# Output projection, first quarter: half of the weight splits moved into it, late ternary tiles on VectorE alone, the next piece's high part moved ahead

## The chip, the cores and the metric

The kernel runs on one core of a Trainium2 chip. The number is the device time of one execution in microseconds (us), shown as the median of several executions. A profiled execution has a time of its own and a span, which is the stretch that its trace covers.

## The reference, cut to what matters

One transformer block on x of shape (2, 1024, 512), with modulation vectors from a small conditioning input. It has two halves:

```
h = layernorm(x) * (1 + ca) + sa
q, k, v = h @ Wq, h @ Wk, h @ Wv          # 32 query heads in 8 groups, one k and v head of 64 for each group
attn = softmax(causal(rope(q) @ rope(k).T / 8)) @ v
x = x + ga * (attn @ Wo)                  # Wo: 2048 x 512, the output projection
h = layernorm(x) * (1 + cb) + sb
x = x + gb * ffn(h)                       # silu(gate) * up, rms norm, down
```

The weights of ffn are quantised to three levels first: w is cast to bf16 and cut in groups of 64; scale = max(mean |w|, 1e-8); w_hat = clip(round(w / scale), -1, 1) * scale; and what is used is w + (w_hat - w), rounded to bf16 at each step.

## The kernel before, in words

**Precision.** The large fp32 products of the attention and of the output projection are made of fp32r products on TensorE: each operand is split into a high part (a cast on ScalarE) and a low part (raw minus high, on VectorE), and high*high, high*low and low*high are added in PSUM. The three product lines of the output projection are L1433, L1434 and L1435.

**Stages.** First the attention, whose step loop runs over 8 head groups with 72 steps each; then the output projection, in four quarters of 512 rows of x; then the feed-forward. The order of work on each engine in the attention is written out by hand: tables at the top give, for each kind of work, the step and the place in the step. Each engine then takes its program strictly in that order, and engines wait for one another on semaphores.

**Splitting Wo.** Wo is 16 tiles of 128 rows, taken two at a time as weight pieces i = 0 to 7. `load_weights` (L1366, issued by SP) loads piece i into `wo_raw[:, i % 2]`, so piece i needs the low part of piece i - 2 to be done; `weights_high` (L1370, ScalarE) makes `wo_hi`, `weights_low` (L1374, VectorE) makes `wo_lo`. The two results lie where `hT_hi` and `hT_lo` were, and the trace calls them that. All eight splits are in the last head group of the attention, at the steps WO_HIGH and WO_LOW (34 to 65), and the loads of pieces 2 to 7 at WO_NEXT.

**The output projection.** A quarter has NPC = 8 pieces s of the attention's output: half i = s // 4 of its rows, and p = s % 4 of the 2048 inner columns, PIECE = 4 tiles each. `load_piece` (L1380, SP) brings a piece to one of O_RING = 4 raw buffers, `piece_high` (L1386, ScalarE) and `piece_low` (L1390, VectorE) split it into one of RING = 2 buffers. `piece_high` of piece s waits until TensorE has finished piece s - 2 (`piece_done`). TensorE does 24 matmuls for a piece (2 row tiles, 4 inner tiles, 3 products), and after pieces 1 to 6 eight transposes (L1446) of a ternary weight tile, which ScalarE copies out (L1515, `copy_turned`). Pieces 0 and 1 of the first quarter are loaded and split while the attention still runs. The first quarter is unrolled (`first`), the other three are a hardware loop. TensorE's first matmul waits for `wo_ready` = 8, all the weights. After half of a quarter VectorE adds the residual (L1536, L1538).

**The late ternary tiles.** The feed-forward's weights are quantised in units of 128x512 beside the attention, six for each head group. Of the last group, units 2 to 5 come in the first quarter of the output projection, at pieces s = 0, 2, 4, 6 (LATE_UNIT_AT). For a unit ScalarE takes |w| (L977) and the sign (L982); VectorE sums the groups (`unit_sum`, L1152); GpSimd makes the scale (L1232); VectorE picks what is over half the scale (`unit_pick`, L1157), which writes `w_hat` and so waits until the unit before has been stored from it; GpSimd multiplies by the scale (L1237), subtracts (L1241), adds (L1245) and puts the sign (L1250); ScalarE issues the store (`unit_store`, L965) just before it takes |w| and the sign of the next unit.

**Order in the first quarter, before.** ScalarE: load of unit 2's weights, two loads of ternary tiles, then for each s: `piece_high(s)` (from s = 2), then, at s = 0, 2, 4, 6, the store of the last unit, |w| and sign of the next and the load of the one after, then `copy_turned`, a ternary load, and at s = 1 and 5 the loads of ga and x (`load_rows`, L1499 and L1500). VectorE: `piece_low(s)` (from s = 2), then at s = 0, 2, 4, 6 `unit_sum` and `unit_pick`, and the residual at s = 4. SP: after the attention's last store (L741) the loads of pieces 4 to 7, each waiting for the low part of the piece four before.

Of the kernel before, what the change touches and what calls it, by code (L numbers as in the profile page):

```python
# [21 lines left out]
ALU = mybir.AluOpType  # L22
# [6 lines left out]
P = 128  # L29
B, S, E = 2, 1024, 512  # L30
T = B * S
H, KVH, D = 32, 8, 64
GQ = H // KVH
HID = 4 * E
QG = 64
# [308 lines left out]
UNITS, UNIT_STEPS = 6, 12  # L344
# [9 lines left out]
ROWS_MOD = ((28, 29, 30, 31), (49, 50, 51, 51), (56, 57, 58, 59))  # L354
ROWS_LOW = ((31, 32, 36, 36), (50, 51, 55, 55), (59, 60, 61, 62))
WO_HIGH, WO_LOW, WO_NEXT = [[at + T for T in (35, 38, 44, 47, 53, 56, 62, 65)] for at in (-1, 0, 1)]
O_LOAD, O_HIGH, O_LOW = 52, (58, 62), (59, 63)
CONSTS_AT, KEYS_AT, QUERIES_AT, QUERY_SWAP, TABLE_AT = 60, 12, 12, 59, 53

# [204 lines left out]
def attention(nc, ps, wq, wk, wv, w_gu, w_p, consts_in, w_in, w_raw, cos, sin, mask, ident, hT_hi, hT_lo, ot_dram, rden_dram,  # L564
# [3 lines left out]
    with ExitStack() as ctx:  # L568
# [163 lines left out]
        def _(sp):  # L732
# [42 lines left out]
            def step(body, T, at):  # L775
                for g, n in body.uses(T, at, SWAPS):
                    swap(g, n)
                for g, n in body.uses(T, at, PLACINGS):
                    place(g, n)
                for g, n in body.whole(T, at, SAVES):  # L780
                    save_den(g, n)
                for g, n in body.whole(T, at, SPREADS):
                    spread_den(g, n)
                for g, n in body.whole(T, at, STORES):
                    store(g, n)
                if at == SP_REST and body.before(T, GATE_STORE):
                    sp.wait_ge(vectors.gates_done, 1)
                    for v in range(2):
                        for n in range(NCH):
                            b = n * B // NCH  # L790
                            sp.dma_start(gates_dram[v, n:n + 1, :], o_sb[b:b + 1, v, :]).then_inc(vectors.gates_out, 16)
                if at == SP_REST and at_last(body, T, WO_LOAD):
                    for i in range(2):
                        outputs.load_weights(sp, i)
                for i in range(2, 8):
                    if at == SP_REST and at_last(body, T, WO_NEXT[i - 2]):
                        outputs.load_weights(sp, i)
                if at == SP_REST and at_last(body, T, O_LOAD):
                    uses_x.await_(sp, body.g, X_HERE - 1)
                    uses_done.await_(sp, body.g, X_HERE - 1)  # L800
                    for buf in range(2):
                        q_place[buf].await_(sp, body.g, 1)
                        sp.wait_ge(o_out[buf], 16 * (PAIRS * (KVH - 1) + PAIRS // 2))
                    for piece in range(O_RING):
                        outputs.load_piece(sp, 0, piece)
                for g, n in body.halves(T, at, WEIGHT_LOADS):
                    sp.wait_ge(w_ready, CT * (g + 1))
                    load_weights(sp, wq, wk, wv, w_raw, w_in, g + 1)
# [143 lines left out]
        def _(act):  # L952
# [61 lines left out]
            def step(body, T, at):  # L1014
# [32 lines left out]
                for g, n in body.uses(T, at, VALUE_HIGHS):  # L1047
# [2 lines left out]
                    tiles_pv.await_(act, g, (36 if unit == 0 else 0) - 1)  # L1050
                    act.copy(v_hl[unit][:, :, 0:D],
                             ps[:, X_BANK, :].rearrange("p (t d) -> p t d", d=D)).then_inc(vhi_ready, 1)
                for i in range(8):
                    if at == ACT_REST and at_last(body, T, WO_HIGH[i]):
                        if i == 0:
                            uses_x.await_(act, body.g, X_HERE - 1)
                        outputs.weights_high(act, i)
# [41 lines left out]
        def _(dve):  # L1099
# [58 lines left out]
                                         scalar=ROUND_HALF, in1=w_abs[:].rearrange("p (g e) -> p g e", e=QG), op0=ALU.mult,  # L1158
                                         op1=ALU.is_lt).then_inc(picked, 1)

            def unit_scales(g, u):
                unit_sum(g, u)
                unit_pick(g, u)

            def late_low(n, k):
                dve.wait_ge(late.h_ready, CT * n + k + 1)
# [3 lines left out]
            def step(body, T, at):  # L1170
                for n in range(1, NCH):
                    if at == 0 and n > 1 and body.before(T, ROWS_STAT[n - 2]):
                        late.statistics(dve, n, late.xt[:, n - 2])
                    if at == 0 and n > 1 and body.before(T, ROWS_NORM[n - 2]):
                        if n == 3:
                            dve.wait_ge(late.tr_done, 3 * CT)
                        late.normalise(dve, n, late.xt[:, n - 2], late.xn)
                    for k in range(CT):
                        if at == 0 and body.before(T, ROWS_LOW[n - 1][k]):
                            late_low(n, k)  # L1180
                for n in range(5):
                    if at == 0 and body.before(T, GATE_STEPS[n]):
                        gate_step(n)
                for g, n in body.uses(T, at, ROTARIES):
                    await_buffer(dve, g, n)
                    rotary_products(g, n)
                for g, n in body.uses(T, at, VALUE_LOWS):
                    unit = X_USES[n][1]
                    v_high.await_(dve, g, V.index(n))
                    dve.tensor_tensor(v_hl[unit][:, :, D:P], ps[:, X_BANK, :].rearrange("p (t d) -> p t d", d=D),  # L1190
                                      v_hl[unit][:, :, 0:D].bitcast(F32), ALU.subtract).then_inc(x_used, 1)
                for g, r in body.rows(T, at, MAXIMA):
                    maximum(g, r)
                for g, t in body.whole(T, at, LOWS):
                    low(g, t)
                for g, n in body.whole(T, at, RECIPROCALS):
                    rows_p.await_(dve, g, 8 * n - 1)
                    if g == 0 and n == 0:
                        dve.wait_ge(pads_ready, 2)
                    dve.reciprocal(rd[:, n % 2, 0:len(ROWS)], den[:, n % 2, :]).then_inc(rd_ready, 1)  # L1200
                for g, n in body.whole(T, at, RECIPROCAL_TURNS):
                    pairs_rd.await_(dve, g, n)
                    pairs_out.await_(dve, g, n - 2)
                    dve.transpose(rd_turned[:, n % 2, :], rd[:, n % 2, :]).then_inc(rd_flipped, 1)
                for g, u in body.units(T, at, UNIT_SUMS):
                    unit_sum(g, u)
                for g, u in body.units(T, at, UNIT_PICKS):
                    unit_pick(g, u)
                for i in range(8):
                    if at == DVE_REST and at_last(body, T, WO_LOW[i]):  # L1210
                        outputs.weights_low(dve, i)
                for piece in range(RING):
                    if at == DVE_REST and at_last(body, T, O_LOW[piece]):
                        outputs.piece_low(dve, 0, piece)
                for g, k in body.halves(T, at, WEIGHT_LOWS):
                    splits_hi.await_(dve, g, 0)
                    dve.tensor_tensor(w_lo[:, k], w_raw[:, k], w_hi[:, k].bitcast(F32), ALU.subtract).then_inc(w_ready, 1)

            bodies(step, ROTARIES, VALUE_LOWS, MAXIMA, LOWS, RECIPROCALS, RECIPROCAL_TURNS, UNIT_SUMS, UNIT_PICKS, WEIGHT_LOWS)
            outputs.vector(dve, unit_scales)  # L1220


        @block.gpsimd
        def _(pool):
# [22 lines left out]
            def unit_signed(g, u):  # L1247
                units_mag.await_(pool, g, u)
                units_sign.await_(pool, g, u)
                pool.tensor_tensor(w_hat[:], w_hat[:], w_sign[:], ALU.mult).then_inc(tern_ready, 1)  # L1250

            UNIT_PARTS = (unit_scaled, unit_difference, unit_magnitude, unit_signed)

            def step(body, T, at):
                for g, n in body.whole(T, at, HALF_SUMS):
# [34 lines left out]
            bodies(step, HALF_SUMS, DIVISIONS, ROTARY_SUMS, KEY_LOWS, QUERY_LOWS, UNIT_SCALES, UNIT_HATS, UNIT_DIFFERENCES,  # L1290
                   UNIT_MAGNITUDES, UNIT_SIGNINGS)

            def unit_rounded(g, u):
                for part in (unit_scale,) + UNIT_PARTS:
                    part(g, u)

            outputs.gpsimd(pool, unit_rounded)

# [7 lines left out]
RING = 2  # L1308
# [32 lines left out]
def project_outputs(nc, ctx, x, wo, tern_gu, tern_p, ot_dram, gates_dram, x2_dram, ident_b, wo_hi, wo_lo, places, wo_raw, wo_in, o_out,  # L1341
# [51 lines left out]
    def sync(sp):  # L1393
        x2_n = x2_dram.rearrange("(n i t p) e -> n p i t e", n=NCH, i=2, p=P)

        def body(n, first):
            for s in range(NPC):
                if not (first and s < O_RING):
                    sp.wait_ge(olo_ready, n * NPC + (s + 1 - O_RING))
# [19 lines left out]
    def tensor(pe):  # L1419
        def body(n, first):  # L1420
            for s in range(NPC):
                i, p = divmod(s, PH)
                if first and s == 0:
                    pe.wait_ge(wo_ready, 2 * PH)
                pe.wait_ge(olo_ready, n * NPC + (s + 1))
                if p == 0 and not first:
                    pe.wait_ge(y_used, 2 * n + (i - 1))
# [23 lines left out]
    def scalar(act, unit_load, unit_parts, unit_store):  # L1451
# [12 lines left out]
        def body(n, first):  # L1464
# [2 lines left out]
                unit_load(KVH - 1, LAST_UNITS)  # L1467
            load_tern(n, 0)
            load_tern(n, 1)
            for s in range(NPC):  # L1470
                if not (first and s < RING):
                    piece_high(act, n, s, first)
                if first and s in LATE_UNIT_AT:
                    u = LAST_UNITS + LATE_UNIT_AT.index(s)
# [42 lines left out]
        chunks(act, body)  # L1517
        rows.root(act, 0)

    def gpsimd(pool, unit_rounded):  # L1520


        pool.memset(free[:], 0.0).then_inc(x2_out[1], 16)
        for u in range(LAST_UNITS, UNITS):
            unit_rounded(KVH - 1, u)

    def vector(dve, unit_scales):
        def add_residual(n, first, i):

            n_ = n if i == 0 else n - 1  # L1530
# [7 lines left out]
            dve.tensor_tensor(x2[:, i], x2[:, i], xt[:, i], ALU.add).then_inc(x2_ready, 1)  # L1538

        def body(n, first):  # L1540
            for s in range(NPC):
                if not (first and s < RING):
                    piece_low(dve, n, s)
                if first and s in LATE_UNIT_AT:
                    unit_scales(KVH - 1, LAST_UNITS + LATE_UNIT_AT.index(s))
                if s == PH:
                    add_residual(n, first, 0)
                elif s == 0 and not first:
# [484 lines left out]
```

## Time and profile before

| | us |
|---|---|
| median of 3 executions | 1734.54 (1732.52 to 1736.47) |
| the profiled execution's own time | 1730.82 |
| its span | 1729.0 |
| TensorE busy | 1675.4, 97% of the span |
| VectorE busy | 1248.8, 72% |
| ScalarE busy | 1140.5, 66% |
| GpSimd busy | 977.1, 57% |
| end of the attention's last product | 1159.6 from the span's start |
| first matmul of the second quarter | 1212.36 |

The engines are PE (TensorE, with PEld for its weight loads), ACT (ScalarE), DVE (VectorE), POOL (GpSimd) and SP, whose queue issues DMAs; a name with q behind it (ACTq, SPq) is an instruction issued by that engine's queue. Times in the rows are counted from the start of the span. A row of the timeline gives the start, the duration, the engine, the line, the operation and what it writes and reads; in brackets stands how long the engine had been idle before it and who released it. Matmuls overlap: one of 512 columns starts 0.23 us after the last at the full clock, though it is shown with 0.39.

### The profile page before, as it was taken

Reading aid. Unit: us, or ns where it says so; the run is one execution under the profiler, and the core shown is the slowest. Engines: PE = TensorE matmul, PEld = TensorE weight load, DVE = VectorE, ACT = ScalarE, POOL = GpSimd, SP = SyncE. Lnnn points to the kernel's source line nnn. Section 1 sums busy time; section 2 is a strip of 40 time slices with the busy share of each in tenths; the row PEclk is TensorE's granted clock in tenths of the full one; section 3 lists DMA queues with packets and bytes.
Section 4 is the critical chain, followed back from the end, with each engine's and each line's share of the span. In section 5 each row is a group of like instructions: output and inputs, shape, how many; then the busy total and the mean of one; then the engine's idle time right before and its main releaser. Section 6 shows DMA issues by size and latency. Waiting matters only on the chain. (4 is left out here: it accounts for less than half of the span.)

```text
span 1729.0 us, 27586 instructions
## 1 busy us (share of the span) xinstructions
PE 1675.4 (97%) x8993; PEld 1386.7 (80%) x8993; DVE 1248.8 (72%) x2518; ACT 1140.5 (66%) x2315; POOL 977.1 (57%) x822
## 2 busy tenths in 40 slices
PE   6899999999999999999999999889999899999998
PEld 2588888888888888888888888667788688888886
DVE  6788889888889888888888988873333564545433
ACT  4588888888888888888888888863232443323222
POOL 1367777777777777777677777445000245444453
PEclk9999999999999999999999999999999999999999
DMA  7234444445445354454354454456555101001000
GB/s 295 71 106 118 131 122 124 122 112 137 112 117 142 99 132 126 103 139 128 96 148 114 107 132 126 132 152 203 188 187 173 53 1 31 25 13 43 0 31 25
DMA packets 174969, 190.92 MB, mean 110 GB/s; under 512 B 31456, under 2 KB 117736, under 8 KB 174832
## 3 DMA queue, kind: packets, MB, share of 16 engines
q1 hardware_dynamic: 137840, 140.99, 28.7%
q10 hardware_dynamic: 36992, 48.25, 10.2%
q8 instruction: 68, 1.11, 0.3%
q14 instruction: 69, 0.57, 0.1%
HBM read 86.12 MB, written 31.74 MB: 68 GB/s over the span
## 5 line engine op out<-in xcount | busy, mean ns | idle before, releaser
L1102 DVE TENSOR_TENSOR p_lo<-ps_b,p_hi 128x512 fp32r<-128x512 f32 x576 | 395.1, 688 | 103.3 <-ACT p_hi L987 99.5
L987 ACT CAST p_hi<-ps_b 128x512 fp32r<-128x512 f32 x576 | 338.2, 589 | 116.3 <-PE ps_b L889 87.7
L1002 ACT ACTIVATE p<-ps_b,negm 128x640 f32<-128x640 f32 (+7 forms) x512 | 382.9, 752 | 41.2 <-DVE negm L1113 39.8
L1113 DVE CUSTOM_DVE_ANT_0 ps_b<-ps_b,mask_w 128x640 f32<-128x640 f32 (+7 forms) x512 | 385.4, 760 | 21.6 <-PE ps_b L878 17.6
L889 PE MATMUL ps_b<-ident,p 128*128 128x128 f32 x2304 | 345.6, 274 | 9.2 <-DVE p_lo L1102 9.1
L889 PEld LDWEIGHTS ps_b<-ident,p 128*128 128x128 f32 x2304 | 271.9, 140 | 56.1 <-DVE p_lo L1102 13.4
L877 PE MATMUL ps_b<-k_hh,q_hl 128*128 128x512 f32 (+3 forms) x768 | 265.6, 347 | 7.5 <-ACT p L1002 6.8
L903 PE MATMUL ps_b<-p_hi,v_hl 128*128 128x512 f32 x576 | 257.9, 448 | 4.0 <-ACT o_sb L995 3.5
L878 PE MATMUL ps_b<-k_l,q_hl 128*128 128x512 f32 (+3 forms) x768 | 256.2, 347 | 0.0
L904 PE MATMUL ps_b<-p_lo,v_hl 128*128 128x512 f32 x576 | 226.6, 393 | 0.0
L1741 PE MATMUL ps_d<-h_hi,gu 128*128 128x512 f32 x512 | 200.6, 392 | 2.4 <-DVE h_lo L1861 2.4
L1742 PE MATMUL ps_d<-h_lo,gu 128*128 128x512 f32 x512 | 199.9, 390 | 0.0
L1257 POOL TENSOR_TENSOR o_sb<-o_sb,o_low 64x512 f32<-64x512 f32 x128 | 164.8, 1292 | 52.0 <-DMA o_low<-o_sb 51.4
L1266 POOL TENSOR_TENSOR rot_c<-rot_c,rot_x 128x512 f32<-128x512 f32 (+1 forms) x96 | 125.7, 1309 | 107.4 <-DMA rot_x<-rot_s 106.8
L877 PEld LDWEIGHTS ps_b<-k_hh,q_hl 128*128 128x128 f32 x768 | 144.7, 188 | 41.7 <-ACT p L1002 9.9
L1262 POOL TENSOR_TENSOR o_sb<-o_sb,rd_all 64x512 f32<-64x512 f32 x128 | 166.5, 1305 | 3.4
L842 PE MATMUL ps_b<-hT_hi,w_hi 128*128 128x512 f32 x384 | 164.1, 427 | 3.7 <-PEq L206 3.2
L878 PEld LDWEIGHTS ps_b<-k_l,q_hl 128*128 128x128 f32 x768 | 144.9, 189 | 28.2
L1837 POOL TENSOR_TENSOR sq<-a 128x512 f32<-128x512 f32 x60 | 70.8, 1180 | 164.2 <-DVE a L1911 163.4
L843 PE MATMUL ps_b<-hT_hi,w_lo 128*128 128x512 f32 x384 | 151.6, 395 | 0.0
L844 PE MATMUL ps_b<-hT_lo,w_hi 128*128 128x512 f32 x384 | 151.3, 394 | 0.0
L1911 DVE TENSOR_TENSOR a<-ps_d,sg 128x512 f32<-128x512 f32 x64 | 44.2, 691 | 140.3 <-PE ps_d L1742 127.4
(160 smaller groups left out, 3123.6 us busy)
## 6 DMA issues: line engine op xcount, KB each, us to landing
rot_x<-rot_s SPq DMA_DIRECT2D x320, 64.0 KB, 2.0
q_hl<-rot_s SPq DMA_DIRECT2D x128, 128.0 KB, 2.6
q_hl<-rot_x SPq DMA_DIRECT2D x128, 128.0 KB, 2.8
rd_all<-reciprocals SPq DMA_DIRECT2D x128, 128.0 KB, 3.0
o_low<-o_sb ACTq DMA_DIRECT2D x128, 128.0 KB, 2.3
attention_out<-o_sb SPq DMA_DIRECT2D x128, 128.0 KB, 2.5
o_raw<-attention_out SPq DMA_DIRECT2D x32, 512.0 KB, 4.7
wf<-in_L_ffn_w_gate_up ACTq DMA_DIRECT2D x28, 256.0 KB, 3.1
```

The source lines that it names most:

```text
L877: pe.matmul(ps[:, bank, 0:n], q, k_hh[unit][:, k0:k0 + n], start=True, stop=False)
L878: ins = pe.matmul(ps[:, bank, 0:n], q, k_l0[:, unit, k0:k0 + n], start=False, stop=True)
L889: ins = pe.transpose(ps[:, T_BANK + T % 2, h * P:(h + 1) * P], p_32[:, parity, h, column * P:(column + 1) * P], ident[:])
L903: pe.matmul(ps[:, O_BANK, :], v_hl[unit][:, j, :], p_hi[:, T % P_RING, :], start=(j == 0), stop=False)
L904: pe.matmul(ps[:, O_BANK, :], v_hl[unit][:, j, :], p_lo[:, T % P_RING, :], start=False, stop=(j == i)).then_inc(pv_done, 1)
L987: act.copy(p_hi[:, T % P_RING, :], ps[:, T_BANK + T % 2, :]).then_inc(phi_ready, 1)
L1002: act.activation(p_32[:, parity, h, column * P:column * P + nk], s, ACT.Exp, bias=negm[:, k:k + 1], scale=-1.0, accum_out=den[:, parity, k ...
L1102: dve.tensor_tensor(p_lo[:, T % P_RING, :], ps[:, T_BANK + T % 2, :], p_hi[:, T % P_RING, :].bitcast(F32), ALU.subtract).then_inc(plo_read ...
L1113: dve.tensor_tensor_reduce(s, s, mask_w[:, S - nk:S], 1.0, HIGHEST, ALU.add, ALU.min, negm[:, k:k + 1]).then_inc(max_ready, 1)
L1262: pool.tensor_tensor(o_sb[0:D, n % 2, :], o_sb[0:D, n % 2, :], rd_all[:, n % 2, :], ALU.mult).then_inc(o_scaled, 1)
L1741: pe.matmul(ps[:, bank + half, :], gu[:, m, half, k, :], h_hi[:, parity, k, :], start=(k == 0), stop=False)
L1742: i = pe.matmul(ps[:, bank + half, :], gu[:, m, half, k, :], h_lo[:, parity, k, :], start=False, stop=(k == CT - 1))
```

## The change

Four edits, all for the last head group and the first quarter.

1. WO_HERE = 4: only weight pieces 0 to 3 are split in the attention, and only pieces 0 to 5 are loaded in it. SP loads pieces 6 and 7 at the start of the output projection, ahead of its loads of attention output; piece 6 needs the low part of piece 4, piece 7 that of piece 5. ScalarE and VectorE split pieces 4 to 7 at the start of the first quarter, ahead of everything else there but ScalarE's three DMA issues.
2. TensorE waits at each of the pieces 0 to 3 of the first quarter for the weights of that piece alone.
3. The late units are done on VectorE alone: sum, scale, pick, product, difference, magnitude, sign in one run, `unit_ternary`. GpSimd has no part in them any more.
4. In the first quarter `piece_high(s + 1)` is issued at s, ahead of the unit work of that s; at s = 2 both pieces 2 and 3 are.

```diff
-                for i in range(2, 8):
+                for i in range(2, WO_HERE + 2):
                     if at == SP_REST and at_last(body, T, WO_NEXT[i - 2]):
                         outputs.load_weights(sp, i)
...
-                for i in range(8):
+                for i in range(WO_HERE):
                     if at == ACT_REST and at_last(body, T, WO_HIGH[i]):
...
+            def unit_ternary(g, u):
+                hat, scales = w_hat[:].rearrange("p (g e) -> p g e", e=QG), gscale[:].unsqueeze(2).broadcast_to([P, NG, QG])
                 unit_sum(g, u)
+                units_sum.await_(dve, g, u)
+                dve.tensor_scalar(gscale[:], gsum[:], 1.0 / QG, 1e-8, ALU.mult, ALU.max).then_inc(gscale_ready, 1)
                 unit_pick(g, u)
+                units_picked.await_(dve, g, u)
+                dve.tensor_tensor(hat, hat, scales, ALU.mult).then_inc(hat_ready, 1)
+                units_hat.await_(dve, g, u)
+                dve.tensor_tensor(w_hat[:], w_hat[:], w_abs[:], ALU.subtract).then_inc(dif_ready, 1)
+                units_dif.await_(dve, g, u)
+                dve.tensor_tensor(w_hat[:], w_abs[:], w_hat[:], ALU.add).then_inc(mag_ready, 1)
+                units_mag.await_(dve, g, u)
+                units_sign.await_(dve, g, u)
+                dve.tensor_tensor(w_hat[:], w_hat[:], w_sign[:], ALU.mult).then_inc(tern_ready, 1)
...
         def body(n, first):
+            for i in range(WO_HERE + 2, 8 if first else 0):
+                load_weights(sp, i)
             for s in range(NPC):
                 if not (first and s < O_RING):
...
-                if first and s == 0:
-                    pe.wait_ge(wo_ready, 2 * PH)
+                if first and i == 0:
+                    pe.wait_ge(wo_ready, 2 * (p + 1))
...
             load_tern(n, 1)
+            for i in range(WO_HERE, 8 if first else 0):
+                weights_high(act, i)
             for s in range(NPC):
-                if not (first and s < RING):
+                if first and s == RING:
+                    piece_high(act, n, s, first)
+                if first and RING <= s < NPC - 1:
+                    piece_high(act, n, s + 1, first)
+                if not first:
                     piece_high(act, n, s, first)
...
         def body(n, first):
+            for i in range(WO_HERE, 8 if first else 0):
+                weights_low(dve, i)
             for s in range(NPC):
                 if not (first and s < RING):
                     piece_low(dve, n, s)
                 if first and s in LATE_UNIT_AT:
-                    unit_scales(KVH - 1, LAST_UNITS + LATE_UNIT_AT.index(s))
+                    unit_ternary(KVH - 1, LAST_UNITS + LATE_UNIT_AT.index(s))
```

## Rows read from the trace of the kernel before

**Rows 1.** The page: busy tenths of TensorE in 40 equal slices.

```profile
PE   6899999999999999999999999889999899999998
```

**Rows 2.** Busy time by stage: PE, PEld, DVE, ACT, POOL (with counts), PEclk, DMA share, GB/s.

```profile
1124.00:1142.00 18.00, 16.62 (x95) 12.98 (x93) 16.87 (x36) 15.70 (x36) 5.95 (x4) 1.00 0.76 234
1142.00:1153.00 11.00, 6.09 (x32) 3.93 (x32) 8.69 (x15) 8.88 (x18) 3.40 (x2) 1.00 0.17 42
...
1181.00:1184.20 3.20, 3.20 (x9) 2.45 (x8) 0.23 (x1) 0.00 (x0) 3.04 (x3) 0.50 0.33 110
```

**Rows 3.** Waits from 1159 to 1232: us in total, times, longest.

```profile
PE ps_c L1433 <- DVE o_lo L1390: 3.9, 2, 2.2
```

**Rows 4.** Timeline of the attention's last steps.

```profile
1141.30 0.65 PE L889 MATMUL ps_b<-ident,p 128*128 128x128 f32 x4 [0.24 <-DVE p_lo L1102]
1141.41 1.03 ACT L1370 CAST hT_hi<-wo_raw 128x1024 fp32r<-128x1024 f32 x1
1143.47 0.50 PE L903 MATMUL ps_b<-p_hi,v_hl 128*128 128x512 f32 x1 [1.52 <-ACT o_sb L995]
...
1146.83 1.26 DVE L1374 TENSOR_TENSOR hT_lo<-wo_raw,hT_hi 128x1024 fp32r<-128x1024 f32 x1
1148.75 0.66 PE L889 MATMUL ps_b<-ident,p 128*128 128x128 f32 x4 [0.65 <-DVE p_lo L1102]
...
1151.52 1.21 DVE L1374 TENSOR_TENSOR hT_lo<-wo_raw,hT_hi 128x1024 fp32r<-128x1024 f32 x1
1153.48 0.63 PE L889 MATMUL ps_b<-ident,p 128*128 128x128 f32 x4 [0.48 <-DVE p_lo L1102]
```

**Rows 5.** Timeline of PE: the first quarter, and the second's first matmul.

```profile
1159.57 0.39 PE L1433 MATMUL ps_c<-hT_hi,o_hi 128*128 128x512 f32 x1
...
1170.89 0.47 PE L1433 MATMUL ps_c<-hT_hi,o_hi 128*128 128x512 f32 x1
...
1176.46 0.62 PE L1446 MATMUL ps_t<-ident_b,w_tern_c 128*128 128x128 bf16 x8
1179.30 0.50 PE L1433 MATMUL ps_c<-hT_hi,o_hi 128*128 128x512 f32 x1 [2.22 <-DVE o_lo L1390]
...
1186.54 0.62 PE L1446 MATMUL ps_t<-ident_b,w_tern_c 128*128 128x128 bf16 x8
...
1212.36 0.49 PE L1433 MATMUL ps_c<-hT_hi,o_hi 128*128 128x512 f32 x1 [1.66 <-DVE o_lo L1390]
```

**Rows 6.** Timeline of SP: the attention's last two stores.

```profile
1161.19 4.71 SPq L741 DMA_DIRECT2D attention_out<-o_sb  x2
```

**Rows 7.** The tile wo_raw, whole run: from the issue of its loads to landing.

```profile
DMA to landing us min/median/max: 3.4/3.7/6.4
```

**Rows 8.** DMA issues from 1166.6 to 1167.5: KB each, median us to landing.

```profile
o_raw<-attention_out SPq DMA_DIRECT2D x2, 512.0 KB, 9.0
```

**Rows 9.** The line of the unit stores, L965, in the first quarter.

```profile
DMA to landing us min/median/max: 1.7/3.3/6.9
```

**Rows 10.** Timeline of ACT and its queue in the first quarter.

```profile
1164.77 0.61 ACT L982 ACTIVATE w_sign<-wf_late 128x512 bf16<-128x512 f32 x1
...
1167.48 1.05 ACT L1386 CAST o_hi<-o_raw 128x1024 fp32r<-128x1024 f32 x1 [2.10 <-issue]
1172.39 0.35 ACTq L965 DMA_DIRECT2D ternary<-w_hat  x1
```

**Rows 11.** Timeline of DVE in the first quarter.

```profile
1177.42 0.69 DVE L1157 SCALAR_TENSOR_TENSOR w_hat<-gscale,w_abs 128x512 bf16<-128x512 bf16 x1 [3.23 <-DMA ternary<-w_hat]
...
1187.53 1.22 DVE L1536 TENSOR_TENSOR x_c<-ps_c,ga 128x1024 f32<-128x1024 f32 x1
...
1189.93 2.18 DVE L1390 TENSOR_TENSOR o_lo<-o_raw,o_hi 128x1024 fp32r<-128x1024 f32 x1
```

**Rows 12.** DVE's groups by shape, whole run: busy, mean ns, idle before.

```profile
L85 DVE TENSOR_SCALAR tmp_d<-tmp_d 128x4 f32<-128x4 f32 x8 | 1.4, 170 | 0.3
...
L1888 DVE COPY wp_last<-wp_b 128x512 bf16<-128x512 bf16 x1 | 0.3, 284 | 0.0
```

More of the change, by code:

```diff
@@ L356 @@
 WO_HIGH, WO_LOW, WO_NEXT = [[at + T for T in (35, 38, 44, 47, 53, 56, 62, 65)] for at in (-1, 0, 1)]
+WO_HERE = 4
 O_LOAD, O_HIGH, O_LOW = 52, (58, 62), (59, 63)
@@ L1159, in unit_pick @@
                                          op1=ALU.is_lt).then_inc(picked, 1)
-            def unit_scales(g, u):
+            def unit_ternary(g, u):
+                hat, scales = w_hat[:].rearrange("p (g e) -> p g e", e=QG), gscale[:].unsqueeze(2).broadcast_to([P, NG, QG])
                 unit_sum(g, u)
+                units_sum.await_(dve, g, u)
+                dve.tensor_scalar(gscale[:], gsum[:], 1.0 / QG, 1e-8, ALU.mult, ALU.max).then_inc(gscale_ready, 1)
                 unit_pick(g, u)
+                units_picked.await_(dve, g, u)
[7 more added lines that the diff above has]
+                dve.tensor_tensor(w_hat[:], w_hat[:], w_sign[:], ALU.mult).then_inc(tern_ready, 1)
             def late_low(n, k):
@@ L1208, in step @@
                     unit_pick(g, u)
-                for i in range(8):
+                for i in range(WO_HERE):
                     if at == DVE_REST and at_last(body, T, WO_LOW[i]):
@@ L1219, in _ @@
             bodies(step, ROTARIES, VALUE_LOWS, MAXIMA, LOWS, RECIPROCALS, RECIPROCAL_TURNS, UNIT_SUMS, UNIT_PICKS, WEIGHT_LOWS)
-            outputs.vector(dve, unit_scales)
+            outputs.vector(dve, unit_ternary)
         @block.gpsimd
@@ L1250, in unit_signed @@
                 pool.tensor_tensor(w_hat[:], w_hat[:], w_sign[:], ALU.mult).then_inc(tern_ready, 1)
-            UNIT_PARTS = (unit_scaled, unit_difference, unit_magnitude, unit_signed)
             def step(body, T, at):
@@ L1291, in _ @@
                    UNIT_MAGNITUDES, UNIT_SIGNINGS)
[L1293 to L1297, printed above, removed]
+            outputs.gpsimd(pool)
 KT = H * D // P
@@ L1518, in scalar, with gpsimd, vector @@
         rows.root(act, 0)
-    def gpsimd(pool, unit_rounded):
+    def gpsimd(pool):
         pool.memset(free[:], 0.0).then_inc(x2_out[1], 16)
-        for u in range(LAST_UNITS, UNITS):
-            unit_rounded(KVH - 1, u)
-    def vector(dve, unit_scales):
+    def vector(dve, unit_ternary):
         def add_residual(n, first, i):
```

## The prediction

> **What bounds the kernel now.** I read the page first: TensorE is busy in nearly every slice [rows 1], so a change beside it is worth only what it takes from, or adds to, TensorE's idle time. Then the busy time by stage: from 1124 to 1142 TensorE lacks 1.4 us, from 1142 to 1153 it lacks 4.9 us, while VectorE and ScalarE are busy about 80% [rows 2]. The waits of the first quarter leave two gaps in front of a piece, both for its low part, 3.9 us together [rows 3]; the timeline puts them at 1179.30 and 1212.36 [rows 5]. Behind the first, the granted clock is 0.50 from 1181 to 1184.2, the lower level of 1.2 GHz [rows 2]: piece 3 takes 7.24 us (1179.30 to 1186.54), piece 2 took 5.57 (1170.89 to 1176.46) [rows 5], so the slow stretch cost 1.7. The second gap, 1.66 us, has no such stretch behind it.
>
> **What goes, in the attention.** Four casts (1.03 each on ScalarE) and four subtractions (1.22 on VectorE) of weight pieces 4 to 7 leave the last steps [rows 4], 9.0 us of engine time, and two DMA issues leave SP. Only what TensorE waited for counts. The cast at 1141.41 stands ahead of a cast and a copy that TensorE waits 1.5 us for; but the transposes that the cast needs end at 1141.95, so 0.35 is gained. The subtraction at 1146.83 stands ahead of the p_lo at 1148.01, and the gap of 0.65 behind it closes; that at 1151.52 holds up the p_lo that TensorE waits for at 1153.48, 0.45 of a gap of 0.48 [rows 4]. The first two pairs (1124 to 1135) lie where TensorE lacks 1.4 us in all; I give them 0.55. Sum 2.0. It is 0 if the chain of one tile after another (transpose, cast, subtraction, product) sets the pace by itself, and at most 3.5, the share of the 6.3 us of gaps with one of the eight in the queue ahead. Minus 2.0.
>
> **What comes, first stall: weight pieces 6 and 7.** TensorE's start on piece 0 (1159.57) is not held: weight pieces 0 to 3 are ready. Its piece 2 started at 1170.89 [rows 5]. Now VectorE must first have done weights_low(4..7), then unit 2, then piece_low(2); and ScalarE weights_high(4..7), |w| and sign, the DMA issues, then piece_high(2). SP reaches the load of weight piece 6 only behind the attention's last store, at 1165.9 [rows 6]; its issue is at 1166.0. The landing is bounded by 3.7, the median of these loads in the quiet attention, and by 9.0, what loads issued at this very place took [rows 7, 8]. I take 6.0: four loads of 512 KB follow one another as before, but those of x and ga come later now. So 1172.0. ScalarE casts pieces 6 and 7 until 1174.0; VectorE is through at 1175.2. ScalarE does |w| and sign until 1175.0 and its DMA issues (2.1, as before the cast of piece 2 at 1167.48 [rows 10]), and piece_high(2) ends at 1178.2. VectorE is later. Its unit: sum 0.72, scale 0.20 (a 128x4 tensor_scalar is 0.17 [rows 12]), pick 0.72 (0.69 [rows 11] and 0.03 for the wait on itself), product 0.72, and three plain bf16 tensor_tensors of 128x512. The trace has none on VectorE. Above stands the pick, 0.69, with two bf16 tensors; below the bf16 copy, 0.28, with one [rows 11, 12]. Neither is clearly nearer; I take the middle, 0.50, and 0.53 with the wait: 1.6. The unit is 4.0, so 1179.2, piece_low(2) 1.2, and TensorE starts piece 2 at 1180.5, 9.6 us later than before. Nothing covers it: pieces 0 and 1 are done at 1170.5.
>
> The Trainium skill, "VectorE: DVE Perf Modes", section "The perf-mode tier table", has a tensor_tensor with bf16 operands in SBUF run at twice the fp32 rate. By that an estimate for the three instructions is about 0.42 each, and the forecast would be about 0.7 us lower over three stalls; no row here shows it.
>
> **Piece 3.** The pick of unit 3 needs unit 2's store: issued 1179.3, landed 4.9 later as in the kernel before (1172.39, pick at 1177.42 [rows 10, 11]), so 1184.2; pick to sign 3.0; piece_low(3) at 1188.4. TensorE does piece 2 in 5.57 and 1.7 for the low clock after so long a gap, then transposes (0.43): 1188.2. Piece 3 starts at 1188.5 and ends at X = 1194.1; before it was 1186.5. The old gap of 2.2 and its slow stretch of 1.7 are in the old figure, so they are paid back here.
>
> **Second stall, in front of piece 5.** Here moving the high part ahead works against the change. At s = 4 ScalarE waits with piece_high(5) for the end of piece 3 on TensorE (X), and behind it in the queue stand the store of unit 3, finished long before, and |w| of unit 4. Cast done X + 1.1, store issued, landed X + 3.7 (1.7 after its issue is the least seen, 6.9 the most, and with few other transfers I take 2.5 [rows 9]); |w| done X + 2.2, sum and scale X + 3.2; pick to sign until X + 6.7; the residual 2.4 (1187.53 to 1189.93 [rows 11]) until X + 9.1; piece_low(5) until X + 10.3. TensorE is through with piece 4 and two sets of transposes at X + 6.4. It idles 4.0 us and pays 1.7 of low clock. Piece 5 runs from 1204.5 to Y = 1211.8.
>
> **Third stall, in front of piece 7.** The same without the residual: piece_high(7) waits for Y, the store lands at Y + 3.7, sign Y + 6.7, piece_low(7) Y + 7.9, against TensorE's Y + 6.4: 1.6 us, short as the old gap at 1212.36, so no slow stretch. Piece 7 ends at 1225.4, and the second quarter follows at once, since unit 5 and its store are over: 1225.5, against 1212.36. Plus 13.1.
>
> **GpSimd** loses its 16 instructions and the one that made the old gaps; what waited for it is counted above. The relaxed wait of TensorE is worth nothing by itself, as without it the whole quarter would wait for pieces 6 and 7. After the first quarter nothing changes.
>
> **Sum.** 13.1 - 2.0 = plus 11.1. The profiled execution took 1730.8 (span 1729.0, 1.8 around it), so 1741.9 for one like it; it lies 3.7 below the median of 1734.5, and for a median I say 1745.5.
>
> **The rivals.**
> *The stalls are there but small.* The weights land in 3.7 (-2.3), the two stores in 1.7 (then the scale is last, -1.0 in all), plain bf16 instructions take 0.28 (-2.0 over three stalls), the attention gives 3.5 (-1.5). Then plus 4.3: 1739. For it: DMA traffic of ga and x is off the place; against: all four at once. Chance 0.20.
> *Transfers collide.* Weights land in 9.0 (+3.0), one of the two stores behind the ga and x loads takes 6.9 (+4.4), the third gap is long enough for a slow stretch (+1.7, less what is regained). Then plus 17 to 20: 1752. Chance 0.16.
> *The attention gives nothing* and the change only moves the splits: plus 13.1, 1747.6. For it: the last tiles are one chain. Chance 0.05.
> *Not slower: VectorE and the weights stay ahead of TensorE.* Place: the start of piece 2. For TensorE not to wait there unit 2 must be finished by 1169.6, so the splits by 1165.6, so weight piece 6 landed by 1162.4. From that point the three stalls go, and so do the old gaps of 2.4 and 1.9 (with their start-up) and the slow stretch: -2.0 - 6.0, 1726.5. Against it: SP cannot issue the load before 1166.0 [rows 6], by the order of its queue; it needs my reading of that order to be wrong. Chance 0.04.
>
> **How the numbers follow.** The forecast has 0.55, with 1741 to 1750 as its own range. From 1738 to 1752 the range takes in the small stalls and part of the collisions. A measurement of this kernel tells 0.2%, 3.5 us, from no change. Faster by that: 0.03, most of the last rival. Within it: 0.04, its rest and the lower end of the small stalls. Slower: 0.93.
>
> **What would show it.** Right: a PE gap of 7 to 12 us in front of piece 2, released by o_lo, with ScalarE waiting there for the landing of wo_raw; then gaps in front of pieces 5 and 7 with ScalarE's store issued just behind piece_high(5) and piece_high(7); clock at 0.50 behind the first two; the attention's last product about 2 us earlier. Wrong: piece 2 following piece 1 at once, or piece 5 starting right behind piece 4; weight piece 6 issued before the last attention store; or an attention whose end does not move.

## The result

| | before | changed |
|---|---|---|
| median, 5 executions each | 1732.52 us (1732.08 to 1736.47) | 1743.60 us (1739.65 to 1746.95) |
| ratio | 1 | 1.0056, 95% interval 1.0040 to 1.0072 |
| profiled execution | 1730.82, span 1729.0 | 1739.65, span 1737.9 |

The change costs 9.7 us by the ratio (6.9 to 12.5) and 8.9 us between the two profiled spans. The prediction forecast 1745.5 against 1734.5, the median of three executions of the kernel before; two more of them brought that median to 1732.52.

The timeline of TensorE in the changed kernel shows where. In these line numbers L1442 to L1444 are the three products of the output projection, L1397 is `piece_low`, L1393 `piece_high`, L1377 and L1381 the splits of the weights, L1373 their load. The first row is a small product of the attention ahead of the removed splits (at 1093.47 in the kernel before). The row at 1156.21 is the first product of the projection, and the transposes at 1189.60 mark the end of piece 3:

```profile
1092.17 0.33 PE L878 MATMUL ps_b<-k_hh,q_hl 128*128 128x128 f32 x1 [0.52 <-ACT p L1003]
...
1156.21 0.39 PE L1442 MATMUL ps_c<-hT_hi,o_hi 128*128 128x512 f32 x1
...
1176.30 0.77 PE L1442 MATMUL ps_c<-hT_hi,o_hi 128*128 128x512 f32 x1 [8.55 <-DVE o_lo L1397]
...
1189.60 0.62 PE L1455 MATMUL ps_t<-ident_b,w_tern_c 128*128 128x128 bf16 x8
...
1198.77 0.50 PE L1442 MATMUL ps_c<-hT_hi,o_hi 128*128 128x512 f32 x1 [2.55 <-DVE o_lo L1397]
...
1213.62 0.50 PE L1442 MATMUL ps_c<-hT_hi,o_hi 128*128 128x512 f32 x1 [2.62 <-DVE o_lo L1397]
...
1220.81 0.39 PE L1442 MATMUL ps_c<-hT_hi,o_hi 128*128 128x512 f32 x1
```

Three gaps, in front of pieces 2, 5 and 7, each released by the low part; those of [rows 5] in front of piece 3 and of the second quarter are gone (the last row follows piece 7 at once). From these rows and [rows 5] the 8.9 us add up: 1.3 gained before any edited instruction (1093.47 against 1092.17; two executions of the same program part), 2.06 gained in the rest of the attention (66.10 from that product to the first of the projection, now 64.04), 11.81 lost in the first quarter (52.79, now 64.60), and the rest, 0.5, lost behind it.

The busy time by stage of the changed kernel shows the clock. It is below 1.00 in the first gap (0.62 over its 8.55 us) and in the first part of piece 2 (0.67 over 5.7 us), and again behind the third gap (0.76 over 7 us), but stays at 1.00 behind the second. There are two levels, 1.00 and 0.50 (2.4 and 1.2 GHz), so a value between them is a stretch with some of each:

```profile
1167.75:1176.30 8.55, 0.00 (x1) 0.04 (x1) 7.15 (x11) 5.94 (x8) 0.00 (x0) 0.62 0.80 272
1176.30:1182.00 5.70, 5.70 (x17) 4.58 (x18) 4.51 (x8) 1.36 (x2) 0.00 (x0) 0.67 0.60 197
...
1198.70:1202.00 3.30, 3.23 (x14) 2.65 (x15) 1.15 (x2) 0.00 (x0) 0.00 (x0) 1.00 0.55 184
...
1214.00:1221.00 7.00, 7.00 (x25) 5.62 (x24) 1.23 (x1) 1.04 (x1) 0.00 (x0) 0.76 0.46 150
```

The first stall, as SP's and ScalarE's timelines show it: SP is at the loads of weight pieces 6 and 7 only after the last stores; ScalarE stands idle 6.56 us for the first to land, with |w| of unit 2 and the high part of piece 2 behind it in its queue.

```profile
1157.77 5.73 SPq L742 DMA_DIRECT2D attention_out<-o_sb  x2
1163.60 1.10 SPq L1373 DMA_DIRECT2D wo_raw<-in_L_attn_Wo  x2
...
1159.20 2.00 ACT L1377 CAST hT_hi<-wo_raw 128x1024 fp32r<-128x1024 f32 x2 [2.20 <-issue]
1167.76 1.04 ACT L1377 CAST hT_hi<-wo_raw 128x1024 fp32r<-128x1024 f32 x1 [6.56 <-DMA wo_raw<-in_L_attn_Wo]
1169.08 1.04 ACT L1377 CAST hT_hi<-wo_raw 128x1024 fp32r<-128x1024 f32 x1 [0.28 <-DMA wo_raw<-in_L_attn_Wo]
1170.03 0.62 ACT L978 ACTIVATE w_abs<-wf_late 128x512 bf16<-128x512 f32 x1
...
1172.62 1.99 ACT L1393 CAST o_hi<-o_raw 128x1024 fp32r<-128x1024 f32 x2 [1.44 <-issue]
```

VectorE then does the splits, the whole of unit 2 and only then the low part:

```profile
1168.83 2.55 DVE L1381 TENSOR_TENSOR hT_lo<-wo_raw,hT_hi 128x1024 fp32r<-128x1024 f32 x2 [4.87 <-ACT hT_hi L1377]
1171.30 0.68 DVE L1153 TENSOR_REDUCE gsum<-w_abs 128x8 f32<-128x512 bf16 x1
...
1172.94 0.69 DVE L1169 TENSOR_TENSOR w_hat<-w_hat,gscale 128x512 bf16<-128x512 bf16 x1
1173.67 0.42 DVE L1171 TENSOR_TENSOR w_hat<-w_hat,w_abs 128x512 bf16<-128x512 bf16 x1
...
1174.93 1.22 DVE L1397 TENSOR_TENSOR o_lo<-o_raw,o_hi 128x1024 fp32r<-128x1024 f32 x1
```

The second and third stall, on ScalarE: `piece_high` waits for TensorE (4.04 and 6.83 us), and right behind it comes the store of a unit that VectorE had finished long before, then |w|, on which VectorE waits for 5.30 us (unit 4) and 6.40 us (unit 5). The store is issued 0.02 us behind the start of the cast in both cases, so it doesn't wait for the cast to end. The pick of unit 4 has no wait of its own; that of unit 5 waits another 2.49 us for its store to land:

```profile
1189.85 1.05 ACT L1393 CAST o_hi<-o_raw 128x1024 fp32r<-128x1024 f32 x1 [4.04 <-PE ps_c L1444]
1189.87 0.36 ACTq L966 DMA_DIRECT2D ternary<-w_hat  x1
...
1204.64 1.05 ACT L1393 CAST o_hi<-o_raw 128x1024 fp32r<-128x1024 f32 x1 [6.83 <-PE ps_c L1444]
1204.66 0.35 ACTq L966 DMA_DIRECT2D ternary<-w_hat  x1
```

```profile
1191.46 0.69 DVE L1153 TENSOR_REDUCE gsum<-w_abs 128x8 f32<-128x512 bf16 x1 [5.30 <-ACT w_abs L978]
...
1192.39 0.69 DVE L1158 SCALAR_TENSOR_TENSOR w_hat<-gscale,w_abs 128x512 bf16<-128x512 bf16 x1
...
1197.50 2.35 DVE L1397 TENSOR_TENSOR o_lo<-o_raw,o_hi 128x1024 fp32r<-128x1024 f32 x2
...
1206.25 0.69 DVE L1153 TENSOR_REDUCE gsum<-w_abs 128x8 f32<-128x512 bf16 x1 [6.40 <-ACT w_abs L978]
...
1209.63 0.69 DVE L1158 SCALAR_TENSOR_TENSOR w_hat<-gscale,w_abs 128x512 bf16<-128x512 bf16 x1 [2.49 <-DMA ternary<-w_hat]
```

### The profile page after: what moved, and what is told of

Read it like the earlier page. It is cut to its first block and busy times, and to the rows that moved or that the text cites. A ratio compares the mean times of both kernels' runs of the same rounds, so it can differ in the third digit from the quotient of the medians.

```text
span 1737.9 us, 27589 instructions
## 1 busy us (share of the span) xinstructions
PE 1679.7 (97%) x8993; PEld 1390.5 (80%) x8993; DVE 1258.6 (72%) x2538; ACT 1140.9 (66%) x2315; POOL 952.2 (55%) x802
## 3 DMA queue, kind: packets, MB, share of 16 engines
q8 instruction: 68, 1.11, 0.3%
```

## The experiments

All ratios are to the kernel before, executed beside them. The runs fall into three groups, on different chips, in which the kernel before had medians of 1734.47, 1733.11 and 1734.60. Two kernels are therefore compared by what each differs from the kernel before (the changed kernel: plus 9.7 us), not by their medians. First each part alone.

**The units alone.** The kernel before with `unit_ternary` and GpSimd's part gone, no other edit.

> Kernel before with the third edit alone: the late units on VectorE. Theory (the loss is in the weight splits and in the order of ScalarE): VectorE's added work is no burden. The gap in front of the second quarter (1.66 us) goes, the gap in front of piece 3 stays at 1.5 to 2.5 us, since the pick of unit 3 still waits for the store of unit 2; 1 to 3 us faster than before. Rival (the loss comes from VectorE taking over GpSimd's work ahead of piece_low): gaps of 2 us or more in front of pieces 5 and 7, and at least 4 us slower than before.

Measured: 1731.12 us, ratio 0.9974 (0.9963 to 0.9984), 4.5 us faster. TensorE's one large gap is in front of piece 3, 2.96 us where 1.5 to 2.5 was expected; VectorE's pick of unit 3 waits 5.50 us for the store of unit 2. PE's row, then DVE's:

```profile
1182.24 0.79 PE L1440 MATMUL ps_c<-hT_hi,o_hi 128*128 128x512 f32 x1 [2.96 <-DVE o_lo L1397]
```

```profile
1178.26 0.69 DVE L1157 SCALAR_TENSOR_TENSOR w_hat<-gscale,w_abs 128x512 bf16<-128x512 bf16 x1 [5.50 <-DMA ternary<-w_hat]
```

The rival falls: VectorE's added work is no burden in the order of the kernel before, and there this part of the change is a gain, larger than the 1 to 3 us expected.

**The splits alone.** The kernel before with WO_HERE = 4, the loads of pieces 6 and 7 by SP and TensorE's wait for each piece.

> Kernel before with the first two edits alone: weight pieces 4 to 7 split in the first quarter, TensorE's wait for each piece. Theory: the first stall comes from here. A gap of 6 to 8 us in front of piece 2 (8.6 in the changed kernel, less some 1.8 of the unit that GpSimd now does), the attention's last product 2 us earlier than before, 6 to 9 us slower than before. Rival (VectorE's unit work makes the stall): a gap under 4 us in front of piece 2 and a time within 3 us of before.

Measured: 1739.95, ratio 1.0028 (1.0017 to 1.0039), 4.9 us slower, less than the 6 to 9 expected. TensorE's two large waits are at 1174.90 and 1217.60, the latter in front of the second quarter, where GpSimd's last chain is (a third one, in front of piece 7, is 0.96 us):

```profile
1174.90 0.77 PE L1436 MATMUL ps_c<-hT_hi,o_hi 128*128 128x512 f32 x1 [7.82 <-DVE o_lo L1391]
...
1217.60 0.76 PE L1436 MATMUL ps_c<-hT_hi,o_hi 128*128 128x512 f32 x1 [3.08 <-DVE o_lo L1391]
```

The stall in front of piece 2 is 7.82 us with the units as before: it belongs to the splits. The 8.55 of the changed kernel is 0.7 more, which leaves little for the unit on VectorE.

**The high part ahead, alone.**

```diff
-                if not (first and s < RING):
+                if first and s == RING:
+                    piece_high(act, n, s, first)
+                if first and RING <= s < NPC - 1:
+                    piece_high(act, n, s + 1, first)
+                if not first:
                     piece_high(act, n, s, first)
```

> Kernel before with the fourth edit alone: piece_high(s + 1) ahead of the unit work of s. Theory: ScalarE holds the unit's store and |w| back until TensorE has finished piece s - 1, so a gap of 1 to 3 us in front of piece 5, and the last unit's chain on GpSimd ends later, with a gap of 3 us or more in front of the second quarter; 3 to 6 us slower than before. Rival (high parts ahead help, as the diff means them to): the gap in front of piece 3 shrinks, nothing new comes, 0 to 2 us faster.

Measured: 1736.55, ratio 1.0012 (1.0003 to 1.0021), 2.1 us slower: the sign is the theory's, the size under its range. PE's three largest gaps are in front of pieces 3 and 5 and of the second quarter; a fourth, in front of piece 7, is 0.88 us:

```profile
1178.99 0.50 PE L1433 MATMUL ps_c<-hT_hi,o_hi 128*128 128x512 f32 x1 [2.48 <-DVE o_lo L1390]
...
1194.34 0.50 PE L1433 MATMUL ps_c<-hT_hi,o_hi 128*128 128x512 f32 x1 [1.53 <-DVE o_lo L1390]
...
1216.27 0.49 PE L1433 MATMUL ps_c<-hT_hi,o_hi 128*128 128x512 f32 x1 [3.09 <-DVE o_lo L1390]
```

**What the splits cost the attention.**

> Kernel before, in which weight pieces 4 to 7 are neither loaded nor split anywhere, and TensorE waits for the first four alone; so half of the output projection's weights are left out. It measures what the splits cost the attention. Theory: the attention's last product ends 2.0 us earlier relative to a product before the splits, and the rest is as before: 2 us faster (0.5 to 3.5). Rival (the last tiles are one chain, the splits lie in its gaps): within 0.5 us of before.

Measured: 1729.84, ratio 0.9973 (0.9963 to 0.9984), 4.7 us faster, more than expected. Between the marked product and the first of the projection lie 63.38 us, 2.7 less than before; the rest of the gain is not placed, since this profile has a gap of 3.10 in front of the second quarter, not 1.66. The other profiles bear the distance out: it is 66.0 to 66.6 us in the four kernels here with all eight splits in the attention. Of the eight with four of them there, seven have 63.4 to 64.0 and one has 65.3. The product's row and that of the first product of the projection:

```profile
1095.14 0.33 PE L878 MATMUL ps_b<-k_hh,q_hl 128*128 128x128 f32 x1 [0.52 <-ACT p L1003]
```

```profile
1158.52 0.39 PE L1434 MATMUL ps_c<-hT_hi,o_hi 128*128 128x512 f32 x1
```

Then each part taken out of the changed kernel.

**Without the high part ahead.** The diff above, undone.

> Changed kernel with the fourth edit undone: piece_high(s) in its old place, behind the unit work of s - 1. Theory (the gaps in front of pieces 5 and 7 come from ScalarE waiting with the high part of the next piece ahead of the unit's store): both gaps, 2.55 and 2.62 us, fall under 1 us, the first stall stays at 7.5 to 9 us; 5 to 8 us faster than the changed kernel, 2 to 5 us slower than before. Rival (VectorE's unit of 3.7 us holds up piece_low by itself): the gaps stay at 2 us or more, and the time within 2 us of the changed kernel.

Measured: 1736.23, ratio 1.0020 (1.0011 to 1.0029), 3.5 us slower than before, so 6.2 faster than the changed kernel. TensorE's waits for the low part are 9.2 us in two places, 8.8 of them in front of piece 2:

```profile
PE ps_c L1442 <- DVE o_lo L1397: 9.2, 2, 8.8
```

The other wait, 0.40 us, is in front of piece 7; in front of piece 5 none is left. The second and third stall are due to the high part's place.

**Without the splits in the quarter.**

> Changed kernel with the first two edits undone: all weights split in the attention as before, units on VectorE, next piece's high part ahead. Theory: the stall of 8.6 us in front of piece 2 goes whole, the attention ends 2.1 us later, a gap of 2 to 3 us comes back in front of piece 3, the two later ones stay; 3 to 5 us slower than before. Rival (VectorE's unit of its own delays piece 2): a gap of 2 us or more stays in front of piece 2.

Measured: 1738.56, ratio 1.0034 (1.0021 to 1.0046), 5.9 us slower, more than the 3 to 5 expected. No gap is left in front of piece 2; those in front of pieces 3, 5 and 7 are 3.48, 2.55 and 1.30:

```profile
1180.59 0.51 PE L1440 MATMUL ps_c<-hT_hi,o_hi 128*128 128x512 f32 x1 [3.48 <-DVE o_lo L1397]
...
1196.94 0.51 PE L1440 MATMUL ps_c<-hT_hi,o_hi 128*128 128x512 f32 x1 [2.55 <-DVE o_lo L1397]
...
1212.08 0.51 PE L1440 MATMUL ps_c<-hT_hi,o_hi 128*128 128x512 f32 x1 [1.30 <-DVE o_lo L1397]
```

This kernel has exactly the third and fourth edit, so it shows how the parts act on one another. Alone they are minus 4.5 and plus 2.1 us, together plus 5.9: 8.3 us more than their sum. Beside the high part ahead, moving the units to VectorE costs 3.8 us instead of gaining 4.5.

**The low part ahead as well.**

```diff
-                if not (first and s < RING):
+                if first and s == RING:
+                    piece_low(dve, n, s)
+                if first and RING <= s < NPC - 1:
+                    piece_low(dve, n, s + 1)
+                if not first:
                     piece_low(dve, n, s)
```

> Changed kernel, and VectorE's piece_low(s + 1) comes ahead of the unit work of s as well, as the high part does. Theory: the low part no longer waits for the unit behind the high part, so the gaps in front of pieces 5 and 7 go entirely though ScalarE's order is the changed one; the first stall stays; 5 to 8 us faster than the changed kernel. Rival (the late store holds up all that follows): the gaps move to the next piece or to the second quarter, at 2 us or more, and less than 3 us is gained.

Measured: 1734.57, ratio 1.0010 (1.0001 to 1.0019): 1.7 us slower than before, so 8.0 faster than the changed kernel. The order on ScalarE is that of the changed kernel, and yet the gaps in front of pieces 5 and 7 are gone; besides the first stall only 0.74 us in front of the second quarter is left. So a wait on ScalarE ahead of the unit hurts only because VectorE had the next low part behind the unit.

```profile
PE ps_c L1442 <- DVE o_lo L1397: 9.4, 2, 8.7
```

**Weight pieces 6 and 7 later**, on top of that. The same two edits stand on VectorE.

```diff
-            for i in range(WO_HERE, 8 if first else 0):
+            for i in range(WO_HERE, WO_HERE + 2 if first else 0):
                 weights_high(act, i)
...
                 if first and s == RING:
                     piece_high(act, n, s, first)
+                    for i in range(WO_HERE + 2, 8):
+                        weights_high(act, i)
```

> As the last kernel, and the splits of weight pieces 6 and 7 come behind the high and low part of piece 2 on ScalarE and VectorE; TensorE needs them at piece 3. Theory (the first stall is ScalarE and VectorE waiting in order for the landing of two loads that TensorE does not need yet): the gap in front of piece 2 falls under 1 us, none of 1 us or more is left in the first quarter, the attention keeps its 2 us; 5 to 10 us faster than before. Rival (the amount of work on VectorE at the start, 2 splits, unit 2 and a low part, is too much in any order): a gap of 3 us or more stays in front of piece 2 or 3, and the time is within 3 us of before.

Measured: 1726.39, ratio 0.9965 (0.9951 to 0.9978), 6.1 us faster than before. The waits for the low part are 13.7 us in the changed kernel and 2.4 here. The longest, 1.14 in front of piece 2, is a little over the 1 us expected:

```profile
PE ps_c L1442 <- DVE o_lo L1397: 2.4, 3, 1.1
```

ScalarE now issues the loads of ga and x (1161.92) ahead of SP's two weight loads (1162.88), and these land later than in the changed kernel. The DMA issues of the changed kernel, then of this one, with the median time to landing:

```profile
wo_raw<-in_L_attn_Wo SPq DMA_DIRECT2D x2, 512.0 KB, 4.5
```

```profile
wo_raw<-in_L_attn_Wo SPq DMA_DIRECT2D x2, 512.0 KB, 7.5
```

**Six pieces in the attention.** As with the low part ahead, and WO_HERE = 6.

> As the kernel with low and high part ahead, but WO_HERE = 6: weight pieces 0 to 5 are split, and all eight loaded, in the attention; the first quarter splits only pieces 6 and 7, whose data are there already. Theory (the landing of loads issued behind the last store makes the first stall, not the splits): no gap of 1 us or more in front of piece 2, about 1 us of the 2 us gained in the attention is given back against the kernel with late pieces 6 and 7; 4 to 7 us faster than before. Rival (splits at the start of the quarter stall TensorE in any case): a gap of 3 us or more in front of piece 2.

Measured: 1727.09, ratio 0.9956 (0.9943 to 0.9969), 7.6 us faster. With data that is there, two splits at the start leave 1.11 us in front of piece 2, a little over the 1 us expected. The rival's 3 us are excluded for two splits, but the run doesn't show that the landing alone makes the first stall, since it takes away two of the four splits as well. The changed kernel's own rows part the 8.55 us: VectorE stands idle for 4.87 of it behind the landing, the two further splits are 2.5 us of work, and 1.1 is what is left here. So by estimate, if the data of all four splits were there, the gap would still be about 3.7 us.

```profile
1171.35 0.47 PE L1442 MATMUL ps_c<-hT_hi,o_hi 128*128 128x512 f32 x1 [1.11 <-DVE o_lo L1397]
```

That two more splits in the attention cost something is not seen: from the marked product to the first of the projection are 63.57 us (1095.14 to 1158.71), as with only four. By this one profile, what the attention gains comes from the splits of pieces 6 and 7, in its last steps.

**One wait for all weights** in the changed kernel, `if first and s == 0: pe.wait_ge(wo_ready, 2 * PH)`.

> Changed kernel with TensorE's wait as it was: at piece 0 for all eight weight pieces. It prices the wait for each piece. Theory: TensorE idles about 15 us in front of piece 0, pieces 0 and 1 no longer lie beside the landing of the weights, but piece 2 then follows without a gap; 4 to 7 us slower than the changed kernel, 13 to 17 slower than before. Rival (the stall is the same wherever it lies): within 2 us of the changed kernel.

Measured: 1749.11, ratio 1.0080 (1.0064 to 1.0096), 13.9 us slower than before, so 4.2 slower than the changed kernel.

```profile
1172.42 0.80 PE L1442 MATMUL ps_c<-hT_hi,o_hi 128*128 128x512 f32 x1 [15.14 <-DVE hT_lo L1381]
```

The wait for each piece does its part: it hides pieces 0 and 1 beside the landing.

**Two refinements of the kernel with late pieces.**

```diff
+                if first and s == 0:
+                    piece_low(dve, n, RING)
                 if first and s == RING:
-                    piece_low(dve, n, s)
```

> As the kernel with late pieces 6 and 7, and VectorE does piece_low(2) ahead of unit 2. Theory: its gap of 1.14 us in front of piece 2 goes, 0.5 to 1.5 us faster than that kernel, 6 to 9 us faster than before. Rival (the store of unit 2, now later, delays unit 3 and piece 3 or 4): a new gap of 1 us or more.

Measured: 1727.61, ratio 0.9961 (0.9948 to 0.9975), not to be told from the kernel with late pieces. The gap moves on to piece 3, as the rival said, but not for its reason: the pick of unit 3 waits 0.24 us for the store of unit 2, while ScalarE waits 6.31 us for weight piece 6 to land, and the low part of piece 3 stands behind the splits of pieces 6 and 7.

```profile
1180.49 0.77 PE L1442 MATMUL ps_c<-hT_hi,o_hi 128*128 128x512 f32 x1 [2.80 <-DVE o_lo L1397]
```

The second one adds `if s % PH == (2 if first and s > PH else 1)` for the loads of ga and x.

> As the last one, and ScalarE issues the second loads of ga and x behind the store of unit 4 instead of ahead of it. Theory (the store queues behind 768 KB of loads, its landing holds up the pick of unit 5): the wait of that pick, 2.4 us, falls under 0.5 us and the 0.8 us in front of the second quarter go; 0.5 to 1.5 us faster than the last one. Rival (the x load then lands too late for the residual): no gain, or a new gap in front of the second pieces of the second quarter.

Measured: 1726.78, ratio 0.9960 (0.9946 to 0.9973), and the pick of unit 5 waits 2.3 us (2.2 in the last kernel):

```profile
DVE w_hat L1158 <- DMA ternary<-w_hat: 2.6, 2, 2.3
```

So those loads are not what makes the store land late; what does is open. The four kernels with late pieces or six in the attention have intervals that overlap: which is best cannot be told, but each is faster than before.

## Why the prediction was right

The time, the sign and all three places were right, and so was the mechanism of each stall. Several terms were off, by up to three microseconds. That the total came within 1.4 us is in part luck: the second stall and its slow stretch were put too high by 3.2 us together, the third stall and its slow stretch too low by 2.6.

- **Attention, minus 2.0.** Measured 2.06 between two profiles. The experiment without the splits gives 2.7 there. The prediction gave 0.55 of it to the splits of pieces 4 and 5; the kernel with six in the attention shows nothing for them.
- **First stall.** Forecast: piece 2 starts 20.9 us after the first product; measured 20.1. SP came to the loads 7.4 us after it (1163.60), not 6.4, but the first landed in time for a cast at 1167.76, 4.2 after its issue, not 6.0. The guess lay too far towards the 9.0 of [rows 8]: ScalarE itself waits for this landing and issues the loads of x and ga only at 1171.58, behind it. The runs bear this out: the two weight loads took 4.1 to 5.1 us to land in all five kernels in which ScalarE waits like this, and 7.2 to 8.8 in the three in which the loads of ga and x go out first. The unit took 3.6 us (1171.30 to 1174.93), not 4.0: the three plain bf16 instructions are 0.42, not 0.50. The estimate that the prediction drew from the Trainium skill, "VectorE: DVE Perf Modes", section "The perf-mode tier table", where a bf16 tensor_tensor runs at twice the fp32 rate, was 0.42, and the trace agrees.
- **Piece 3.** Forecast to start 0.3 late, it followed at once: the store of unit 2 had landed by the pick at 1177.29, 2.3 us after its issue (1175.04), not 4.9. Low clock was paid as forecast, piece 2 taking 7.3 us (1176.30 to 1183.60).
- **Second stall.** Forecast 4.0 us and 1.7 of low clock, measured 2.55 and none. The store went out at X + 0.3, beside the cast and not behind it, so VectorE's pick at X + 2.8 did not wait for it: X + 3.7 was too late by a microsecond, and the cheaper unit gave most of the rest. Why the clock held is not shown. The length of the gap does not decide it: gaps of 2.22 us (the kernel before) and of 2.55 us (without the splits in the quarter, and with one wait for all weights) had a slow stretch behind them, one of 2.60 us (half of the weights left out) had none.
- **Third stall.** Forecast 1.6 and no low clock, measured 2.62 and low clock. The store landed 5.0 us after its issue (1204.66 to the pick at 1209.63), not 2.5; why is open. Second and third together: 7.3 forecast, 5.2 and a slow stretch of 1.6 measured (piece 7 took 7.19 us, piece 5 took 5.62).
- **The old gaps** went as forecast, that in front of the second quarter for the reason given (the experiment with the units alone has none there either).
- **GpSimd** lost 20 instructions (five for each unit), not 16; no term of the sum rests on it.
- **The quarter**: plus 13.1 forecast, plus 11.8 measured; the sum of all, 11.1 against 9.7 by the ratio.
- **The rivals.** "The attention gives nothing" is excluded by 2.06 and 2.7. "Not slower" needed VectorE ahead of TensorE at piece 2, and its point of decision was the right one: of the kernels with splits in the quarter, only those that lift the landing out of that queue beat the kernel before. It put the gain at 8.0 us; the kernel with late pieces gained 6.1, the one with six pieces in the attention 7.6. Of the two rivals on size each had a part right: the weights landed in 4.2 us and the pick of unit 4 did not wait for a store, towards small stalls; the store of unit 4 took 5.0 us and the third gap had a slow stretch, as when transfers collide.

The prediction did not say that the parts cost less apart than together: plus 4.9, plus 2.1 and minus 4.5 sum to 2.5, the whole is 9.7. Nearly all of that lies between the third and the fourth edit: together they are plus 5.9, and the splits add 3.8 to them, less than the 4.9 that they cost alone. A reading that fits is that with GpSimd doing the units only `unit_sum` and `unit_pick` stood on VectorE ahead of the next low part, and with the whole unit there each wait of ScalarE holds up more. The kernel with the low part ahead supports it, since it takes away 8.0 us with ScalarE's order unchanged; it was not tested further.

## What to carry to other kernels

Work moved from a stage where the engines are full to one where they idle helps only if nothing in front of it in their queues waits: a split whose data is loaded behind the last store of the stage before belongs behind everything that TensorE needs earlier. If one half of a pair is put ahead of other work (here the high part on ScalarE), the other half, on VectorE, must be put ahead too, or the wait is only passed on. When a change of several parts loses, measure each alone and also what the others do without it: here moving the units to VectorE gains 4.5 us by itself, and costs 3.8 beside the high part ahead.

## What was not expected of the hardware

A bf16 tensor_tensor of 128x512 on VectorE takes 0.42 us with two plain operands, but 0.69 when one is the scale spread over 64 elements, with the same types and shape (the rows L1171 and L1169 above). The groups of VectorE by shape, from 1155 to 1222 us of the changed kernel, also show the low part at its bare 1.22 us in all seven cases where GpSimd is idle, while the four weight splits, two of them beside GpSimd's last work for the attention, average 1.55:

```profile
L1397 DVE TENSOR_TENSOR o_lo<-o_raw,o_hi 128x1024 fp32r<-128x1024 f32 x7 | 8.5, 1220 | 5.5 <-ACT o_hi L1393 5.5
L1381 DVE TENSOR_TENSOR hT_lo<-wo_raw,hT_hi 128x1024 fp32r<-128x1024 f32 x4 | 6.1, 1552 | 9.7 <-ACT hT_hi L1377 9.6
```

And two gaps of nearly the same length, 2.55 and 2.62 us, left the clock at its upper level once and not the other time. Whether that makes executions differ was not tested; those of the changed kernel spread over 7 us (1739.65 to 1746.95), and so did eleven of the kernel before (1730.92 to 1738.20).
